# Taking the row maximum off the attention scores in one pass of four 32-row matmuls instead of two passes of 64-row ones

## The reference

```python
scores = jnp.einsum('bhnd,bhmd->bhnm', q, k) / jnp.sqrt(jnp.float32(hd))
attn = jax.nn.softmax(scores, axis=-1)
out = jnp.einsum('bhnm,bhmd->bhnd', attn, v)
out = out.transpose(0, 2, 1, 3).reshape(B, H * W, C)
out = out @ w_o + b_o
```

## Time and profile before

| | |
|---|---|
| median of 3 runs | 4373.63 us (4372.26 to 4374.09) |
| the profiled execution, its own time | 4372.58 us |
| its span, first to last instruction | 4370.9 us |
| PE matmul busy | 4039.6 us (92%) |
| PE weight load busy | 2426.7 us (56%) |
| DVE busy | 2652.2 us (61%) |
| ACT busy | 1933.8 us (44%) |
| POOL busy | 2668.0 us (61%) |
| the four kinds of passes on L1123, busy | 408.8, 407.0, 405.8 and 404.4 us |
| mean granted TensorE clock | 0.978 of full speed |

### The profile page before, as it was taken

One profiled execution on the slowest core, in us unless ns is written; L12 is line 12 of the kernel. 1 busy time (PEld: TensorE's weight loads), 2 busy tenths in 40 slices (PEclk: granted clock), 3 DMA queues, 4 the chain that ended last, 5 costly groups with the idle time before them and its releaser, 6 DMA issues.

```text
span 4370.9 us, 69097 instructions
## 1 busy us (share of the span) xinstructions
PE 4039.6 (92%) x21822; PEld 2426.7 (56%) x21822; DVE 2652.2 (61%) x2771; ACT 1933.8 (44%) x3504; POOL 2668.0 (61%) x1303
## 2 busy tenths in 40 slices
PE   0599989999999989999899998999989998999989
PEld 0355646565465655656465564656546565565645
DVE  4446684557736676465854658455773667646585
ACT  0145453544535445354534545355452544535453
POOL 0167376755758458584676737676575845858467
PEclk9899999999999999999999999999999999999999
DMA  7211212112131211212121121211203121121212
GB/s 273 87 37 49 95 43 95 54 71 73 34 105 44 80 54 56 88 51 87 54 96 41 45 99 39 98 54 61 82 32 108 44 80 54 54 91 51 87 52 83
DMA packets 147413, 314.94 MB, mean 72 GB/s; under 512 B 17600, under 2 KB 30400, under 8 KB 136512
## 3 DMA queue, kind: packets, MB, share of 16 engines
q1 hardware_dynamic: 147008, 309.92, 20.7%
HBM read 259.54 MB, written 50.33 MB: 71 GB/s over the span
## 4 chain that ended last, share of the span: by engine, by line
PE 82%; DVE 9%; issue 4%; DMA 3%; ACT 1%; SPq 0%; DVEq 0%; POOL 0%; ACTq 0%
PE aux_ps L1035 29%; PE acc_ps L1137 20%; PE score_ps L1123 19%; PE aux_ps L1076 8%; PE score_ps L1035 3%; DVE mxp L944 3%; PE aux_ps L1147 2%; DMA xin<-in_x_dram 1%; DMA w_split<-o_t 1%; DVE sc L812 1%; PE aux_ps L1085 1%; DVE sc L819 1%; DVE sc L820 0%; DVE den L972 0%; DVE xin L905 0%
## 5 line engine op out<-in xcount | busy, mean ns | idle before, releaser
L588 POOL TENSOR_TENSOR sums<-sums,probs 128x1024 f32<-128x1024 f32 x768 | 1867.4, 2432 | 892.5 <-ACT probs L714 852.2
L944 DVE TENSOR_REDUCE mxp<-aux_ps 128x2 f32<-128x1024 f32 x1041 | 1274.0, 1224 | 1218.5 <-PE aux_ps L1076 1205.1
L714 ACT ACTIVATE probs<-score_ps 128x512 f32<-128x512 f32 x2048 | 1056.9, 602 | 663.9 <-PE score_ps L1123 656.0
L1137 PE MATMUL acc_ps<-probs,v_y 128*64 128x512 f32 x4096 | 1017.6, 618 | 0.0
L1035 PE MATMUL aux_ps<-xs,w_qk 128*128 128x512 f32 x3168 | 871.0, 414 | 40.8 <-DMA w_qk<-w_split 40.8
L1035 PEld LDWEIGHTS aux_ps<-xs,w_qk 128*128 128x128 f32 x3168 | 572.4, 192 | 465.0 <-issue 301.7
L588 POOL TENSOR_TENSOR sums<-probs 128x1024 f32<-128x1024 f32 x128 | 305.2, 2384 | 538.4 <-ACT probs L714 538.4
L1076 PE MATMUL aux_ps<-k_hi,q_hi 64*128 64x512 f32 x2082 | 481.2, 456 | 159.0 <-DVE mxp L944 153.1
L1137 PEld LDWEIGHTS acc_ps<-probs,v_y 128*64 128x64 f32 x4096 | 251.6, 138 | 477.4 <-issue 438.6
L972 DVE RECIPROCAL den<-den 128x256 f32<-128x256 f32 (+1 forms) x240 | 443.9, 1849 | 7.7 <-ACT den L725 7.7
L1123 PE MATMUL score_ps<-q_hi,k_hi 64*128 64x512 f32 x2048 | 408.8, 395 | 20.6 <-issue 20.6
(11 more groups left out here) (114 smaller groups left out, 3377.9 us busy)
## 6 DMA issues: line engine op xcount, KB each, us to landing
xin<-in_x_dram SPq DMA_DIRECT2D x280, 256.0 KB, 2.9
w_qk<-w_split SPq DMA_DIRECT2D x134, 512.0 KB, 4.1
w_v<-w_split SPq DMA_DIRECT2D x34, 1024.0 KB, 6.8
w_o<-w_split SPq DMA_DIRECT2D x32, 1024.0 KB, 7.1
w_split<-o_t SPq DMA_DIRECT2D x16, 1024.0 KB, 5.5
y<-v_y SPq DMA_DIRECT2D x64, 256.0 KB, 2.0
v_y<-in_x_dram SPq DMA_DIRECT2D x64, 256.0 KB, 2.8
xin<-y SPq DMA_DIRECT2D x64, 256.0 KB, 2.7
```

What stands on the lines that cost most here:

```text
L588: pool.tensor_tensor(sums[h][:, :], a, probs[:, g % SLOTS_P, :], ALU.add).then_inc(c_sum[h].sem, 1)
L714: act.activation(probs[:, n % SLOTS_P, token_half(u % 2)], score_ps[:, u % SCORE_BANKS, :], ACT.Exp, scale=SCALE).then_inc(c_exp.sem, 1)
L944: dve.tensor_reduce(mxp[:, :, n, h], ps, AX.X, ALU.max).then_inc(c_free["D"].sem, 1)
L1137: last = nc.tensor.matmul(acc_ps[head(j), :], v_y[:, m, head(2 * p + j)], probs[:, n % SLOTS_P, token_half(j)], start=(m == 0), stop=(m == ...
```

## The change

`scores` loses its fourth pass and no longer tells ACT anything. A new function `less_max` sends, once a batch, four matmuls of 32 rows, one for each of the four score banks, on the partitions 0 to 31, 32 to 63, 64 to 95 and 96 to 127; each tells `c_score`. It stands behind the second `max_slot` and ahead of `prob_v`. For this minus the maximum must stand in four rows, 0, 32, 64 and 96: `first_row` gets four rows of ones, `combine` writes `mxw` in 32 places instead of 16, `neg_rows` sends 97 columns instead of 65, and ACT copies 97 rows.

```diff
@@ tables and buffers @@
+QUARTER = P // 4
+ROWS_M = 3 * QUARTER + 1
-        mxw = sb("mxw", [P, NT, 66], F32R)
+        mxw = sb("mxw", [P, P], F32R)
@@ gpsimd, once @@
-            pool.memset(first_row[0:1, :].bitcast(F32), 1.0).then_inc(s_const, 1)
-            pool.wait_ge(s_const, 7)
-            pool.memset(first_row[HD:HD + 1, :].bitcast(F32), 1.0).then_inc(s_const, 1)
-            pool.wait_ge(s_const, 8)
+            for q in range(4):
+                pool.memset(first_row[q * QUARTER:q * QUARTER + 1, :].bitcast(F32), 1.0).then_inc(s_const, 1)
+                pool.wait_ge(s_const, 7 + q)
@@ scalar, neg_rows @@
-                    act.activation(q_max[0:HD + 1, p % 2, token_half(h)], ps[0:HD + 1, :],
-                                   ACT.Copy).then_inc(c_free["A"].sem, 1)
+                    act.activation(q_max[0:ROWS_M, p % 2, token_half(h)], ps[0:ROWS_M, :], ACT.Copy).then_inc(c_free["A"].sem, 1)
@@ vector, combine @@
-                for j in range(2):
-                    dve.tensor_reduce(mxw[:, :, HD * j], mxp[:, j, :, :], AX.X, ALU.max,
+                quarters = mxw[:, :].rearrange("p (j r c) -> p j r c", j=2, r=2)
+                for r in range(2):
+                    dve.tensor_reduce(quarters[:, :, r, 0:NT], mxp[:, :, :, :], AX.X, ALU.max,
                                       negate=True).then_inc(c_mx.sem, 1)
@@ tensor @@
-                        last = nc.tensor.matmul(ps[0:HD + 1, n * P:(n + 1) * P], mxw[:, 4 * h + n, 0:HD + 1],
+                        last = nc.tensor.matmul(ps[0:ROWS_M, n * P:(n + 1) * P], mxw[:, 4 * h + n:4 * h + n + ROWS_M],
                                                 ident[:, :], start=True, stop=True)
...
-                        todo = ((k_hi, q_hi), (k_lo, q_hi), (k_hi, q_lo), (first_row, q_max))
-                        for s, (kk, qq) in enumerate(todo):
+                        for s, (kk, qq) in enumerate(((k_hi, q_hi), (k_lo, q_hi), (k_hi, q_lo))):
                             for j in range(2):
-                                lhs = kk[head(j), :] if kk is first_row else kk[head(j), p % 2, keys]
-                                last = nc.tensor.matmul(score_ps[:, (2 * n + j) % SCORE_BANKS, :], lhs,
-                                                        qq[head(j), p % 2, cols], start=(s == 0), stop=(s == 3))
-                                if s == 3:
-                                    last.then_inc(c_score.sem, 1)
+                                nc.tensor.matmul(score_ps[:, (2 * n + j) % SCORE_BANKS, :], kk[head(j), p % 2, keys],
+                                                 qq[head(j), p % 2, cols], start=(s == 0), stop=False)
+
+                    def less_max(b):
+
+                        p, h = b // 8, (b // 4) % 2
+                        for u in range(4):
+
+                            first = HD * (u % 2) + QUARTER * (u // 2)
+                            quarter = slice(first, first + QUARTER)
+                            nc.tensor.matmul(score_ps[:, u, :], first_row[quarter, :], q_max[quarter, p % 2, token_half(h)],
+                                             start=False, stop=True).then_inc(c_score.sem, 1)
...
                         scores(2 * b + 1)
                         max_slot(i, t, *max_slot_at(b, 1))
+                        less_max(b)
                         if b:
                             prob_v(2 * b - 2)
```

More of the change, by code:

```diff
@@ L548, in _ @@
             pool.memset(ones[:, :], 1.0).then_inc(s_const, 1)
-            pool.memset(mxw[:, :, :].bitcast(F32), 0.0).then_inc(s_const, 1)
+            pool.memset(mxw[:, :].bitcast(F32), 0.0).then_inc(s_const, 1)
             pool.memset(q_max[:, :, :].bitcast(F32), 0.0).then_inc(s_const, 1)
@@ L562, in _ @@
                                pattern=[[-GROUP, P // GROUP], [0, GROUP]], channel_multiplier=1).then_inc(s_const, 1)
-            pool.wait_ge(s_const, 10)
+            pool.wait_ge(s_const, 12)
             pool.affine_select(out=g3, in_=g3, compare_op=ALU.is_ge, fill=0.0, base=GROUP - 1,
@@ L797, in _ @@
                                   ALU.subtract).then_inc(s_split, 1)
-            dve.wait_ge(s_const, 11)
+            dve.wait_ge(s_const, 13)
             dve.tensor_copy(ident[:, :], den[:, 0, 0:P]).then_inc(s_ident, 1)
@@ L1025, in _ @@
         def _(pe):
-            pe.wait_ge(s_const, 11)
+            pe.wait_ge(s_const, 13)
             pe.wait_ge(s_ident, 1)
```

## The result

The changed kernel takes 4559.6 us (median of 4 runs, 4557.1 to 4563.78) against 4373.66 us. The ratio is 1.0427, 95% interval 1.0409 to 1.0445: 4.3% slower, +186 us, where +153 was forecast.

What follows compares the result with a forecast made beforehand. PE was taken to bound most batches; 125 + 20 + 12 - 4 = +153 us on 4372.6 us gave 4526 us, 3.5% slower. The forecast's own range was 4495 to 4560 us, the wider one 4415 to 4590.

Steps and rivals of the forecast that it cites:

- The bound: PE bounds most batches; its passes between the slots just cover DVE's first-slot read, with 0.01 to 0.07 us slack.
- Part 1: Two score passes less between the two slots of the maxima: 0.15 us won, not 0.46, in each of 417 batches.
- Part 2: The group of four 32-row matmuls behind the second slot adds 0.46 us, between bounds of 0.23 and 0.69.
- Part 3: neg_rows loads 97 columns in place of 65: 0.21 us more in 56 batches, +12 us.
- Part 4: First batch of a branch: one pass less brings the first slot forward 0.23 us, 16 times, 4 us won.
- What costs nothing: ACT's exponentials, POOL and the masks move later under cover; DVE's mask waits may cost a few us, combine under 2.
- No drain: Behind the second slot, 64 to 32 rows costs no switch; the group takes 0.23 us: +51, 4424 us; chance 0.14.
- Not side by side: The four matmuls go two by two, a second pass in 460 batches: +106 us on the forecast, 4632 us; chance 0.09.
- Faster: PE's sum of passes decides, 8 become 7: -0.23 us in each of 460 batches, about 4274 us; chance 0.03.

Runs made afterwards that it cites:

- half reads: DVE's reduction of the maxima reads the first 256 of 512 columns: on the kernel before 4312.1 us, on the changed kernel 4355.7 us.
- small sums: POOL's sums cover 8 columns instead of 1024: kernel before 4224.6 us, the same with ACT's exponentials late 4230.0 us, changed kernel 4409.5 us.

## Why the prediction was right, and where it was off

- **The bound.** That DVE's read of the first slot, with 0.07 us of slack, sets the second slot: right. Waiting slots went from 107 to 524, with 0.43 us each in the ordinary batch, and with half reads the loss of the ordinary batches was gone. The loads stand where the forecast put them, but for `prob_v`: 0.88 us after the second slot where 0.9 to 1.0 was said.
- **Part 1**, 0.15 us a batch for two passes: right, a little small: 0.17 measured; alone it gave -60 us where -51 was worked out.
- **Part 2**, 0.46 us for the group: 0.43 measured. A batch changed by +0.27, not +0.30. The sum of the two was mis-sized by some 12 us in the direction of too slow.
- **Part 3**, +12 us: 3 to 12 measured; the loads of one `neg_rows` grew by 0.20 us against 0.21, its batch by 0.18.
- **Part 4**, -4 us for the first batches: wrong. In its place stand +24 us. The step counted passes and not the clock at which they run: the two first batches lose 27 us more to it than before.
- **What costs nothing.** "POOL and the masks for the next branch move by the same 1.3 us and wait for ACT either way; DVE's waits for those masks may cost a few us" is the step that failed in kind. The cover for PE held: scores never waited for ACT. But the sums were seen as work that is free wherever it lies. Moved onto DVE's small steps, they hold them up: 75 us in the run that did this alone, 22 of them as a lower clock. In the changed kernel batches 1 to 7 of branch 1 have 18 us over PE's term, and with small sums nearly all of that was gone.
- **The rivals.** No drain: out, the 32-row load comes 0.45 after the slot. Not side by side: out, one group takes 0.43. Faster: out for want of slack, and even with it (half reads) the changed kernel is 44 us behind.

The two misses outweigh the overestimate of parts 1 and 2, and so 186 came where 153 stood: 153 - 12 + 28 + 18 = 187. That this closes so well is in part luck, since batches 13 to 31 of branch 1, and the time lost to the clock in them, were not taken apart. No version that beats the kernel before came out of this without giving up part of the result.

## What to carry to other kernels

Before taking passes out of a matmul engine's row, find what else ends at the same point. Here eight passes covered one read of two banks with 0.07 us to spare, and two passes less bought only a wait. A group of small row tiles pays a switch of about one pass (0.18 to 0.2 us here), so four tiles in one pass are worth it only where they replace more than two passes; a place in which the group needs no switch of its own was not tried. And where work that is off the chain moves, ask what it will then run beside. Before a difference in one stage is put down to a mechanism, compare the granted clock of that stage in both runs.

## What was new about the hardware

- DVE's small steps (`tensor_tensor`, `scalar_tensor_tensor`, `tensor_scalar` of 128 x 128) take 0.23 to 0.29 us and up to 2.44 when they meet a POOL sum of two SBUF tensors; with sums of 8 columns in its place every one is back at 0.23 to 0.29 in the lines shown. The whole kernel before got 148 us shorter with them, some 66 of these through the granted clock. The Trainium skill, SBUF — State Buffer, SBUF: two separate sides, says that the two engines share a pair of ports under an exclusive lock held for the whole instruction; the trace agrees, with 2.40 and 2.44 us, and the step ends 0.15 us or less after the sum.
- A 64-row pass followed by a 32-row one: 0.45 us between the loads, against 0.11 for a 64-row one behind a slot that waited. Four 32-row matmuls side by side take what two 64-row ones do, 0.43 against 0.46 us for a lone pass.
- A delay of about 1 us on an engine with 44% busy time cost 1.7% of the run, about a third of it through the granted clock, without one instruction more and with PE's program unchanged.
